# First attention of a four-layer kernel: 50 contracted rows a head without blanked rows, parts stored in stack order, loads of 48 partitions

## The reference

```python
x = L0_attn_in_features                       # (2, 2048, 256) float32
n = _layernorm(x)
q, k, v = (_proj_heads(n, w, 16) for w in (q_proj_weight, k_proj_weight, v_proj_weight))   # (2, 16, 2048, 16)
scores = jnp.einsum('bhqd,bhkd->bhqk', q, k) / sqrt(16) + causal_mask
out = jnp.einsum('bhqk,bhkd->bhqd', jax.nn.softmax(scores), v)
x = x + jnp.einsum('bsv,mv->bsm', merge_heads(out), o_proj_weight)
```

## Time and profile before

| what | value |
|---|---|
| median of 3 runs | 1893.46 us (1889.39 to 1895.38) |
| the profiled execution's own time | 1889.35 us |
| its span, first to last instruction | 1887.2 us |
| mean granted TensorE clock | 0.935 of full speed |
| bytes moved by DMA | 125.92 MB |
| phase_qkv with its barrier and the jump over phase_shift | up to 135.3 us |
| first attention's first scores | 138.9 us |

### The profile page before, as it was taken

One profiled execution on the slowest core, in us unless ns is written; L12 is line 12 of the kernel. 1 busy time (PEld: TensorE's weight loads), 2 busy tenths in 40 slices (PEclk: granted clock), 3 DMA queues, 4 the chain that ended last, 5 costly groups with the idle time before them and its releaser, 6 DMA issues. The chain is left out here.

```text
span 1887.2 us, 30933 instructions
## 1 busy us (share of the span) xinstructions
PE 1632.7 (87%) x10275; PEld 1117.3 (59%) x10276; DVE 933.1 (49%) x1799; ACT 961.2 (51%) x1531; POOL 474.8 (25%) x510
## 2 busy tenths in 40 slices
PE   5938999999999985999829999999758986898898
PEld 4722223222222224888718888888647976797787
DVE  6623434424425434777653333333275555665785
ACT  3537999999999972444332222222123334333342
POOL 3113112111111111455642222222123103000665
PEclk9968999999999996999969999999968997898999
DMA  4756156156236008321131111111132010000001
GB/s 162 202 179 80 21 77 83 32 69 86 42 56 86 18 13 293 125 84 37 66 123 48 50 50 50 52 51 50 39 101 69 22 41 16 1 1 4 23 23 45
DMA packets 75081, 125.92 MB, mean 67 GB/s; under 512 B 11168, under 2 KB 45600, under 8 KB 71840
## 3 DMA queue, kind: packets, MB, share of 16 engines
q1 hardware_dynamic: 67872, 103.51, 23.5%
q0 software_dynamic: 7104, 21.01, 3.7%
HBM read 74.63 MB, written 49.85 MB: 66 GB/s over the span
## 5 line engine op out<-in xcount | busy, mean ns | idle before, releaser
L685 ACT ACTIVATE probs<-ps_s 128x1024 f32<-128x1024 f32 (+3 forms) x640 | 514.1, 952 | 46.2 <-PE ps_s L731 43.4
L748 PE MATMUL ps_o<-probs,V 128*17 128x512 f32 (+3 forms) x2560 | 298.4, 537 | 9.4 <-POOL probs L673 8.3
L673 POOL TENSOR_SCALAR_AFFINE_SELECT probs<-probs 128x512 f32<-128x512 f32 x128 | 86.7, 680 | 460.3 <-ACT probs L685 456.8
L731 PEld LDWEIGHTS ps_s<-Q_even,K_even 64*128 64x128 f32 x640 | 56.2, 188 | 154.2 <-ACT probs L685 127.3
L1362 DVE COPY slot_hT<-ps_hT 128x512 f32<-128x512 f32 x72 | 49.8, 691 | 195.2 <-PE ps_hT L1405 195.2
L731 PE MATMUL ps_s<-Q_even,K_even 64*128 64x512 f32 (+3 forms) x640 | 127.6, 447 | 21.6 <-DMA Q_even<-shift_parts 13.9
L698 DVE COPY weighted<-ps_o 128x512 f32<-128x512 f32 x32 | 22.1, 690 | 249.8 <-PE ps_o L748 249.8
L705 DVE RECIPROCAL inv_denominator<-ps_o 128x512 f32<-128x512 f32 x32 | 107.4, 3358 | 73.9 <-PE ps_o L762 73.9
L731 PEld LDWEIGHTS ps_s<-Q_odd,K_odd 64*128 64x128 f32 x640 | 55.1, 183 | 139.6 <-ACT probs L685 126.4
L1415 PE MATMUL ps_slot_y<-we_out,slot_hT 128*128 x576 | 136.3, 380 | 0.9 <-DVE slot_hT L1362 0.9
L1884 POOL TENSOR_TENSOR h_lo<-h,h_hi 128x512 fp32r<-128x512 f32 x64 | 89.4, 1413 | 183.8 <-DVE h L1930 183.8
(11 more groups left out here) (281 smaller groups left out, 3990.3 us busy)
## 6 DMA issues: line engine op xcount, KB each, us to landing
slot_rows<-slots_in SPq DMA_DIRECT2D x72, 128.5 KB
qk_parts<-qk_hi SPq DMA_DIRECT2D x8, 1024.0 KB, 4.3
qk_parts<-qk_lo SPq DMA_DIRECT2D x8, 1024.0 KB, 7.1
Q_odd<-qk_parts SPq DMA_DIRECT2D x24, 256.0 KB
K_odd<-qk_parts SPq DMA_DIRECT2D x24, 256.0 KB
Q_even<-qk_parts SPq DMA_DIRECT2D x18, 256.0 KB
K_even<-qk_parts SPq DMA_DIRECT2D x18, 256.0 KB
X<-x SPq DMA_DIRECT2D x8, 512.0 KB, 4.3
```

The lines of the kernel that those rows point to most:

```text
L673: pool.affine_select(out=block_of, in_=block_of, compare_op=ALU.is_ge, fill=0.0, base=0, pattern=[[0, HG], [1, P]], channel_multiplier=-1) ...
L685: act.activation(probs[:, at % PROB_BUFS, 2 * p:2 * p + 2, off:BT], ps_s[:, s % SCORE_BUFS, :, off:BT], ACT.Exp).then_inc(exp_ok, 1)
L731: last = pe.matmul(ps_s[:, s % SCORE_BUFS, h, off:BT], K[j][HALF * h:HALF * h + HALF, p, t * P:(t + 1) * P], Q[j][HALF * h:HALF * h + HALF ...
L748: last = pe.matmul(ps_o[32 * h:32 * h + DH + 1, q % 2, off:BT], k["V"][:, group, SEQ_TILES * b + t, h, :], probs[:, at % PROB_BUFS, h, off ...
```

## The change

The scratch tensor in DRAM is laid out as the stacks are: for Q three slots of parts (high, high, low), for K (high, low, high), 48 rows one behind the other. phase_qkv therefore stores high parts twice: a quarter's store is one slot, 8 heads of 16 rows by 512, and a block has 12 of them, issued quarter by quarter, 256 KB each. A load fetches the 48 rows of a side in one piece, 4 loads of 768 KB a unit. The shift rows follow at row 48, so the scores contract 50 rows; nothing else of the 64 rows is read, and no row is blanked. K's two rows of ones come from a small DRAM tensor that POOL's ones are stored to (load_ones, twice 2 partitions). In phase_shift the loop over row tiles on TensorE becomes a register loop with the query tile copied by VectorE first, which makes its code short: 64 groups of matmuls in the program become 2. The core of the diff, in the order of the file: constants, SP, POOL and ScalarE of phase_qkv, the two load functions, SP, POOL and TensorE of phase_attention, and the scratch tensors:

```diff
-SHIFT_ROWS, SHIFT_PARTS = 2 * DH, 2
-SLOT_ROWS = (0, DH, 3 * DH)
+STACK_ROWS = 3 * DH
+SHIFT_PARTS = 2
+USED_ROWS = STACK_ROWS + SHIFT_PARTS
 Q_SLOTS, K_SLOTS = (0, 0, 1), (0, 1, 0)
-STACK_LOADS = 2 * (len(Q_SLOTS) + len(K_SLOTS))
+STACK_LOADS = 4
...
+                sp.wait_ge(ones_ok, 1)
+                sp.dma_start(io["ones"].rearrange("m p t -> (m p t)").rearrange("(p n) -> p n", p=P), ones[:, :]
+                             ).then_inc(ones_out, 16)
                 for b in range(BLOCKS):
                     j = b % 2
                     t0 = b * BT % SEQ
-                    for n, (part, done) in enumerate(((qk_hi, hi_ok), (qk_lo, lo_ok))):
-                        sp.wait_ge(done, 4 * b + 4)
-                        to = io["qk"][n, b * BT // SEQ, :, :, :, t0:t0 + BT].rearrange("m (c g) r t -> (g r) (m c) t", c=DC)
-                        sp.dma_start(to, part[:, j].bitcast(F32)).then_inc(parts_out[j], 16)
+                    for m, slots in enumerate((Q_SLOTS, K_SLOTS)):
+                        to = io["qk"][m, b * BT // SEQ].rearrange("(c g) p s r t -> c r (g p s) t", c=DC)
+                        for wanted, part, done in ((0, qk_hi, hi_ok), (1, qk_lo, lo_ok)):
+                            for c in range(DC):
+                                sp.wait_ge(done, 4 * b + DC * m + c + 1)
+                                for row, slot in enumerate(slots):
+                                    if slot == wanted:
+                                        sp.dma_start(to[c, DH * row:DH * row + DH, :, t0:t0 + BT].rearrange("d h t -> h d t"),
+                                                     part[:, j, DC * m + c].bitcast(F32)).then_inc(parts_out[j], 16)
...
                 pool.memset(zeros[:, :], 0.0).then_inc(zero_ok, 1)
-                pool.wait_ge(zero_ok, 1)
-                pool.wait_ge(w_lo_ok, 3)
-                blank_rows(pool, k["first_stacks"][0], k["first_stacks"][1], 1.0, blank_ok)
+                pool.memset(ones[:, :], 1.0).then_inc(ones_ok, 1)
                 for parity in range(2):
-                    pool.wait_ge(parts_out[parity], 32 * (SEQ // BT // 2))
+                    pool.wait_ge(parts_out[parity], 16 * STORES * (SEQ // BT // 2))
                 load_stacks(pool, io, 0, 0, k["first_stacks"][0], k["first_stacks"][1], k["first_in"])
...
-                    wait_past(act, parts_out[j], 32 * n)
+                    wait_past(act, parts_out[j], 16 * STORES * n)
...
+def load_ones(eng, io, K, sem):
+
+    for side in range(2):
+        at = HALF * side + STACK_ROWS
+        eng.dma_start(K[at:at + SHIFT_PARTS].bitcast(F32), io["ones"]).then_inc(sem, 16)
+
+
+def load_stacks(eng, io, g, b, Q, K, sem):
+
+    for m, stack in enumerate((Q, K)):
         for side in range(2):
-            at = HALF * side + SHIFT_ROWS
-            pool.memset(stack[at:at + SHIFT_ROWS].bitcast(F32), value).then_inc(sem, 1)
-            pool.wait_ge(sem, 2 * n + side + 1)
+            src = io["qk"][m, b, bass.ds(g, 1)].rearrange("o p s r t -> s r (o p) t")[side]
+            at = HALF * side
+            eng.dma_start(stack[at:at + STACK_ROWS].bitcast(F32), src).then_inc(sem, 16)
...
                 load_shifts(sp, 0, 0)
-                sp.wait_ge(blank_ok, 4)
+                load_ones(sp, io, K[1], ones_in)
                 load(sp, 1, 1)
...
-                blank_rows(pool, Q[1], K[1], 1.0, blank_ok)
                 pool.memset(pick_f32[:, :, :], 0.0).then_inc(pick_ok, 1)
...
-                                             K[j][HALF * h:HALF * h + HALF, p, t * P:(t + 1) * P],
-                                             Q[j][HALF * h:HALF * h + HALF, p, q * BT + off:(q + 1) * BT],
+                                             K[j][HALF * h:HALF * h + USED_ROWS, p, t * P:(t + 1) * P],
+                                             Q[j][HALF * h:HALF * h + USED_ROWS, p, q * BT + off:(q + 1) * BT],
...
-    io["qk"] = scratch("qk_parts", (2, BATCH, 2, GROUPS, HG * DH, SEQ), F32)
+    io["qk"] = scratch("qk_stacks", (2, BATCH, GROUPS, 2, 2, STACK_ROWS, SEQ), F32)
+    io["ones"] = scratch("key_ones", (SHIFT_PARTS, 2, SEQ), F32)
```

More of the change, by code:

```diff
@@ L244, in phase_qkv @@
         over = sb("over", [1, 2, 8], F32)
+        ones = sb("ones_fill", [P, 2 * SHIFT_PARTS * SEQ // P], F32)
         zeros = sb("shift_zeros", [P, HEADS * TOK * SHIFT_PARTS // P], F32)
@@ L493, in phase_shift @@
         ps_t = mem.enter_context(nc.psum_tensor("ps_top", [HG * QT, P], F32))
-        loaded, scores_ok, mask_ok, blank_ok, masked_ok, top_ok, turned_ok, neg_ok, split_ok, stored, parts_free = sems(
-            k, "shift", "loaded scores_ok mask_ok blank_ok masked_ok top_ok turned_ok neg_ok split_ok stored parts_free")
+        stage = sb("query_tile", [P, P], F32R)
+        loaded, stage_ok, scores_ok, mask_ok, masked_ok, top_ok, turned_ok, neg_ok, split_ok, stored, parts_free = sems(
+            k, "shift", "loaded stage_ok scores_ok mask_ok masked_ok top_ok turned_ok neg_ok split_ok stored parts_free")
         EACH = HG * QT
@@ L546, in _ @@
                     with dve.Fori(0, UNITS) as u:
-                        for h in range(HG):
+                        for pair in range(2):
                             with dve.Fori(0, QT) as t:
[L549 to L556, removed]
+                                hold(dve, k, loaded, 16 * STACK_LOADS * (u + 1))
+                                for at in (0, HALF):
+                                    dve.tensor_copy(stage[at:at + STACK_ROWS, :],
+                                                    Q[at:at + STACK_ROWS, pair, bass.ds(t * P, P)].bitcast(F32)
+                                                    ).then_inc(stage_ok, 1)
+                                for side in range(2):
+                                    at = EACH * u + 2 * QT * pair + 2 * t + side
+                                    hold(dve, k, scores_ok, at + 1)
+                                    hold(dve, k, top_ok, at + 1)
+                                    dve.tensor_tensor(masked[:, :], ps_s[:, :], mask[:, bass.ds(SEQ - P - P * t, SEQ)],
+                                                      ALU.add).then_inc(masked_ok, 1)
+                                    hold(dve, k, masked_ok, at + 2)
+                                    dve.tensor_reduce(top[:, bass.ds(QT * (2 * pair + side) + t, 1)], masked[:, :], AX.X,
+                                                      ALU.max).then_inc(top_ok, 1)
                         dve.wait_ge(turned_ok, u + 1)
@@ L570, in _ @@
                     with pe.Fori(0, UNITS) as u:
[L571 to L579, removed]
+                        for pair in range(2):
+                            with pe.Fori(0, QT) as t:
+                                hold(pe, k, loaded, 16 * STACK_LOADS * (u + 1))
+                                hold(pe, k, stage_ok, 4 * QT * u + 2 * QT * pair + 2 * t + 2)
+                                for side in range(2):
+                                    hold(pe, k, masked_ok, EACH * u + 2 * QT * pair + 2 * t + side + 1)
+                                    at = HALF * side
+                                    for c in range(0, SEQ, BT):
+                                        last = pe.matmul(ps_s[:, c:c + BT], stage[at:at + STACK_ROWS, :],
+                                                         K[at:at + STACK_ROWS, pair, c:c + BT], start=True, stop=True)
+                                    last.then_inc(scores_ok, 1)
                         hold(pe, k, top_ok, EACH * u + EACH + 1)
@@ L618, in phase_attention @@
         stored = sems(k, "rows_stored", "even odd")
[L619 to L620 removed]
+        ones_in, pick_ok, zero_ok, scores_ok, exp_ok, mask_ok, pv_ok, sums_ok, picked_ok, norm_ok, result_ok = sems(
+            k, "attention", "ones_in pick_ok zero_ok scores_ok exp_ok mask_ok pv_ok sums_ok picked_ok norm_ok result_ok")
         def group_and_batch(u):
```

23 lines of the change are left out of this document (9 added, 14 removed).

## The result

The changed kernel takes 1913.5 us (median of 4 runs, 1912.07 to 1917.71) against 1893.1 us before: 1.0113 times the time, 95% interval 1.0099 to 1.0128. The second rival, eight engines at full speed, had said 1923.

What follows compares the result with a forecast made beforehand. TensorE, with waits for DMA, was taken to bound the projection, ScalarE's exponents attention; the new stores would set the projection's pace. +101 - 2 - 9 = +90 us on 1889.35 gave 1979, stated as 1980 us; range 1915 to 2015.

Steps and rivals of the forecast that it cites:

- second rival: Projection stores: 8 engines at full speed, 185 GB/s, stores take 136 us, sum +30, 1923 us; chance 0.22.
- rate of the new stores: Projection stores: 16.5 GB/s an engine, 132 GB/s, 25.2 MB in 191 us, 23.8 us a block.
- width: Projection stores: 8 outermost on one side and 128 on the other, so 8 engines take part.
- first rival: Projection stores take all 16 engines, 8.3 us a block at 380 GB/s, hidden; -20, 1873 us; chance 0.14.
- third rival: Projection stores: engines in step crowd the same SBUF entrances, 119 GB/s, 212 us; +116, 2009 us; chance 0.10.
- Loads 17 us: The first attention unit's loads, half through the same 8 engines as the stores: 17 us, between 8.5 and 19.5.
- Landing 2 us: End of the projection phase: landing of the last store takes 2 us.
- End of phase +101: Projection's last store lands at 21 + 191 + 17 + 2 = 231 us against 130.1: +101 us.
- short branch -2: Barrier after the jump, where SP waits 3.4 us for TensorE: bounds 0 and -3.4, taken as -2 us.
- Start of attention -9: First attention: without POOL's blanking of Q_odd and K_odd the 9.62 us gap nearly closes, -9 us (-8 to -10).
- memset term: Block 0 of the projection: 9.7 us of VectorE regained from POOL's memsets, but behind the stores, so counted as nothing.
- Two of its signs: Projection profile: ScalarE waits some 12 us in each of blocks 2 to 7; TensorE busy well under half, often at half clock.

Runs made afterwards that it cites:

- kernel 5: The changed kernel with the first unit's loads held until all eight blocks are stored; 1922.5 us in one run.
- kernel 6: The changed kernel with narrow stores kept but each high part stored once, 8 stores a block and 8 loads a unit; 1876.55 us, ratio 0.9934.
- kernel 1: The changed kernel with the stack's DRAM rows ordered row by row, slot inside, so stores have 128 outermost on both sides; 1858.83 us, ratio 0.9863.
- kernel 3: The kernel before with each 1 MiB store cut into eight of 16 partitions, same bytes; 1895.49 us in one run.
- kernel 4: The kernel before with the short branch alone, register loops in phase_shift; 1883.17 us, ratio 0.9978.
- kernel 2: The changed kernel with the stores and twelve loads of before, slots at rows 0, 16, 32; 1871.33 us, ratio 0.9908.
- kernel 7: The changed kernel with two wide 1 MiB stores a block, high parts stored once, rows interleaved in DRAM, 10 loads a unit; 1862.29 us, ratio 0.9854.

## Why the prediction was wrong, step by step

**The rate of the new stores is the step that failed.** "I take the nearest row with few engines, 16.5 GB/s each: 132 GB/s, 25.2 MB in 191 us, 23.8 us a block." Measured: 204 GB/s, 24 GB/s for each engine's busy time (204/(0.53 x 16)), 15.4 us a block, 123.4 us in all. Kernels 5 and 6 show the same 204 with the loads away and with a third fewer bytes, and kernel 1 gives each of its 16 engines the same 24. The two rows it was taken from were a 1 us window of a 32 KB load and a window of 32 KB stores; the 1 MiB stores, 23 GB/s an engine, were the right row. Why the other two are slow is not shown: in those stores an engine has 2 KB to move, but the load gives each of its two engines 16 KB, as much as a store of kernel 1 gives, and it differs in direction and rows as well. Nor was 8 x 23.1 = 185 GB/s the upper bound that it was called, since 204 is 10% above it: the 23.1 is for each engine's busy time at a share of 1.03 and was multiplied by 8 engines at a share of 0.50; the trace reads 0.53, and 24 instead of 23.1. I had even counted the 2 KB packets that the new stores share with them, and gave that its weight in rival 2 only. The prediction also named 119 GB/s from the 16-row loads as a bound and "an engine slows where few partitions are touched at a time" as the reason: kernel 3 shows 208 GB/s out of 16 partitions, so the 121 GB/s is no bound for stores out of them.

**The width was right.** The share is 0.53, eight engines, though 128 partitions stand on the SBUF side; the first rival (1873 us) is out, and kernel 1 shows what it would have been worth. That follows the rule of the Trainium skill ("DMA: Bandwidth & Descriptors", section "Why a DMA increments its semaphore by 16 and not by 1"), the largest number up to 16 that divides both outermost counts; the trace agrees, 0.53 for 8 and 128, 1.03 for 128 and 128.

**The third rival** (2009 us) needed engines that crowd the same entrances of SBUF. The Trainium skill's port rule ("SBUF — State Buffer", section on the DMA port swizzle), by which I had worked out 109 GB/s, did not come out: 204 GB/s. The 121 GB/s of the 16-row loads, which the prediction took as agreeing with four ports, lie above those 109 as well and are weak support for them. Why the eight engines don't crowd is not settled; that they drift apart was not tried.

**The other terms.** Stores from 21.0 us: 21.5. Loads 17 us: 11 by kernel 5, within the 8.5 to 19.5 given, nearer to the end for full speed; why was not tried. Landing 2 us: the phase ends at 164.8, so behind 21.5, 123.4 and 11 some 9 us are left; kernel 5 has most of them too (153.3 - 22.0 - 123.4 = 7.9). The landing itself is some 2 of them (in kernel 5 DMA moves 12 GB/s from 152 us on), part are blocks that begin below the full rate, and the rest is not traced. End of phase +101: measured +34.7, the 66 us between them being 8 blocks x (23.8 - 15.4) = 67; that loads 6 us too long and an end 7 us too short cancel is luck. The short branch -2: -2.9 (kernel 4: -3). Start of attention -9: -8.4, and half a microsecond of it back at the first scores. The memset term held: VectorE's normalisation in block 0, 11.11 us before, reads after

```profile
20.24 1.38 DVE L217 TENSOR_SCALAR xn<-X,ln_moments,ln_rstd 128x256 f32<-128x256 f32 x4
```

and it counts for nothing behind the stores, but shows in kernel 2. Scores over 50 rows, ones for K_odd and later loads: 0, and the spans' difference leaves no room for more.

So the mechanism, eight engines that make the stores the pace of the phase, was the one forecast; what it costs at the end of the phase was taken 2.9 times too large (101 for 34.7 us), by a rate from the wrong rows. Two of its signs went wrong with the rate: ScalarE waits 5 to 6 us a block and not 12, and until 92 us TensorE is busy 49.7 of 64 us at a granted clock of 0.92; only from 120 to 160 us is it under half, 15.7 of 40 us, at 0.71.

**A version that beats both.** Kernels 1 and 7 take 0.986 and 0.985 of the time of before, 1859 and 1862 us. Kernel 1 is the change with one thing altered, the order of a stack's 48 rows in the scratch tensor.

## What to carry to other kernels

A layout that makes a load wide can make the store narrow: look at the outermost count of both sides of every transfer, and put the dimension that is long on both sides outermost. For its rate, take the nearest row of the same direction that is alike in packet size and in what an engine gets, not that of a transfer that merely has as few rows or engines. And multiply width by bytes before giving a verdict: half as many bytes more hid under the compute when the stores were wide (kernel 1), eight engines nearly did with the bytes of before (kernel 6, 14 us behind its wide twin, kernel 7), and only with both does the phase end 35 us later than before.

## What the runs showed of the hardware

- Transfers of 16 rows into SBUF go at 121 to 125 GB/s, of 48 rows at 152 to 160, all at a share of 0.99 or more, while reads out of SBUF in groups of 16 partitions ran at 204 (8 engines) and 208 GB/s. Direction is the likely cause, but not shown: these loads also move rows of 8 KB in one piece and the stores runs of 2 KB.
- A queue that is full holds its issuer: SP's issue was 0.37 us for a 1 MiB store before and is some 1.28 us for a 256 KB store, exactly the time of one such store at 204 GB/s; in kernel 1, at 393 GB/s, four issues take 2.7 us, again the stores' own time; and two took 18.8 us in kernel 6 while loads filled the engines. Whatever stands behind it on SP waits as well.
- Loads issued by POOL in the midst of stores hold back the stores issued after them: ScalarE stops for 13 to 20 us in the kernels with wide stores, for 20 us in the changed kernel and 25 in kernel 6, where stores are narrow. Alone, behind all stores (kernel 5), the same loads take some 21 us.
